# Attention stack as one pipeline over tiles and layers, rotation from PSUM, norms by logarithm

## The chip, the core and the metric

One core of one Trainium2 chip runs the whole program. Five engines work beside each other: PE (TensorE, matrix products and transposes), DVE (VectorE), ACT (ScalarE), POOL (GpSimd) and SP (SyncE, which issues the DMAs here). Each runs its own list of instructions in order and waits on semaphores that others raise. The metric is the time of one execution in microseconds (us); lower is better.

## The reference

The input is 4 batches of 512 tokens with 128 channels, in float32. The model is `x = x + mamba(norm(x))`, then `x = x + stack(norm(x))`, then `x = x + topk_attention(norm(x))`, then `x = x + stack(norm(x))` again with the same weights. Only `stack` concerns the change:

```python
for i in range(6):
    x = attn_layer(shift_tokens(x), Wqkv[i], q_scale[i], k_scale[i], Wo[i]) + x
    x = ffn_layer(shift_tokens(x), ln_g[i], ln_b[i], W1[i], b1[i], W2[i], b2[i]) + x
# attn_layer, 16 heads of 64, windows of 32 tokens; a window sees itself and the one before
q, k = l2norm(q) * qs, l2norm(k) * ksc
q = q * cos * scale + rotate_half(q) * sin * scale      # k the same, with 1 / scale
out = local_attention(q, k, v)                          # softmax over at most 64 keys
# ffn_layer: a norm over the channels, 128 -> 2 x 341, a * gelu(gate), 341 -> 128
```

`shift_tokens` takes the second half of the channels from the token before. `l2norm` divides the 64 numbers of a head by the root of the sum of their squares.

## The kernel before, in words

`ffn_stack` (line 334) is called twice, as f0 and f1, with all activations resident in SBUF (channels on the partitions: `XA` holds a layer's input, `XB` its value after attention). A layer has 16 tiles of 128 tokens, 4 in each batch. In every engine's program `steps` (line 380) runs through the tiles: 4 steps written out, a hardware loop of three rounds of 4 steps, and 3 steps at the end. In the step `kk` four tiles are in work at four stages: projection, rotation and norm of tile `kk`; turning (transposing) of Q and K and the scores of tile `kk-1`; softmax, product with V and division of tile `kk-2`; output projection and residual of tile `kk-3`.

In one step:

- PE projects Q, K and V in six units of 512 columns through PSUM banks 0 and 1 in turn (line 454 for Q and K, 460 for V), multiplies with Wo (line 492), turns prob (465) and Q and K (473), forms PV (line 527) into banks 6 and 7 and the scores (536, 541) into banks 4 and 5, and turns the attention output (551). All turns go through banks 2 and 3.
- ACT copies each unit and each turned bank to SBUF (line 600, `raw`, `v_tok`, `probT`, `qT`, `kT`, `oT`), squares Q and K (619), makes the exponential (645) and the shifted input of the next tile (704, 705).
- DVE rotates from the copies: cos times `raw` (line 771) and sin times `raw` with its halves exchanged (775, two instructions of 512); it sums the squares (797), finds the inverse root by a shifted integer guess and three Newton rounds on 128x32 (754 to 764), sums the softmax (783), divides (808), finds the row maximum (816) and subtracts it (819).
- POOL adds the two halves of the rotation (879), multiplies by the inverse root (882) and adds the residual (874).
- SP issues 20 small DMAs per tile that spread V over the windows, and four weight loads per layer.

When all 16 tiles of a layer are through, the feed-forward part of the layer runs by itself: DVE makes `xn`, the norm's mean, variance and inverse root pass through PE, ACT (Square and Sqrt) and DVE, then for each batch three pairs of products (line 579), Gelu on ACT (726), a product on DVE (854), the output products (565), and DVE adds bias and `XB` into `XA` (844). ACT changes its function table at each of Sqrt, Gelu and Exp (line 719 and its neighbours). The next layer starts when this is over.

Of the kernel before, what the change touches and what calls it, by code (L numbers as in the profile page):

```python
# [333 lines left out]
def ffn_stack(k, a, phase):
    nc = k.nc
    with ExitStack() as ctx:
        s = names(ctx, phase, nc, *LN_SEMS, "wqkv_in", "wo_in", "w12_in", "tabled", "zeroed", "xs_ready", "proj_full", "proj_evac", "v_in_even", "v_in_odd",
                  "sq_done", "ss_done", "newton", "rn_ready", "rope_added", "rot_done", "add_done", "t_full",
                  "t_evac", "scores", "top", "sub_done", "exp_done", "summed", "rden_done", "pv_done", "on_done",
                  "wo_done", "res_done", "shifted", "gate_full", "gate_evac", "val_full", "val_evac", "out_full", "out_evac", "scrap")  # L340
# [29 lines left out]
        warm = sb("warm", [P, 1])  # L370

        xn = raw[:, :, :, :].rearrange("p a h e -> p (a h e)").rearrange("p (b n) -> p b n", b=B)
        k.ln_sq = sq[:, 0, :, :].rearrange("p h e -> p (h e)").rearrange("p (i n) -> p i n", i=2)
        k.ln_std = sq[:, 1, 0:4, :].rearrange("p h e -> p (h e)").rearrange("p (i n) -> p i n", i=2)
        gate = t2[:, 0, :, :].rearrange("p h e -> p (h e)").rearrange("p (i n) -> p i n", i=2)
        hid = rope[:, :, :, :, :].rearrange("p a c h e -> p (a c h e)").rearrange("p (i c n) -> p i c n", i=2, c=4)
# [3 lines left out]
        def steps(eng, fn, L):  # L380

            for j in range(4):
                fn(L, 0, j, j)
            with eng.Fori(1, B) as b:
                for j in range(4):
                    fn(L, b, j, 4 * b + j)
            for j in range(3):
                fn(L, B, j, LT + j)

        def tile(x, r0, r1, b, t0, n=P):  # L390
            if isinstance(b, int):
                return x[r0:r1, b, t0:t0 + n]
# [1236 lines left out]
```

## Time and profile before

| | us |
|---|---|
| median of 3 runs | 7111.84 (7104.78 to 7119.3) |
| profiled execution | 7122.96, of which the span is 7121.2 |
| PE busy | 5984.3 (84%) |
| DVE busy | 5970.1 (84%) |
| ACT busy | 3439.2 (48%) |
| POOL busy | 2652.3 (37%) |
| mean granted clock of TensorE | 0.931 of full |

Busy time is that of one engine, so the columns overlap; the span is the time from the first instruction to the last. The two stacks take most of the span, and in each of them six layers with the same two stages (attention steps, then the feed-forward part) alternate. PEclk is the clock that TensorE was granted: 1.00 is 2.4 GHz, 0.50 is 1.2 GHz. An idle time in brackets names the instruction whose end released the waiting one.

### The profile page before, as it was taken

The page shows a single profiled execution, that of the slowest core. Times are in us where ns is not written, and L with a number is a line of the kernel's source. Part 1 is how long each engine was busy: PE and PEld are TensorE (multiplying, and loading weights), DVE is VectorE, ACT ScalarE, POOL GpSimd, SP SyncE. Part 2 cuts the span into 40 slices and gives each one's busy share as a digit, 9 for nine tenths or more (in the row PEclk, how much of TensorE's full clock was granted, in tenths as well). Part 3 has the DMA queues.
Part 4 walks back from the last instruction along what each step waited for, and adds up shares of the span by engine and source line. Part 5 has one row for each costly group of instructions (what it writes and reads, how often), then busy time and mean ns, then how long its engine had stood idle before and what let it go on. Part 6 is the DMA issues. An engine that isn't in the chain of part 4 may idle for free. (4 is left out here: it accounts for less than half of the span.)

```text
span 7121.2 us, 150074 instructions
## 1 busy us (share of the span) xinstructions
PE 5984.3 (84%) x47596; PEld 3842.3 (54%) x47596; DVE 5970.1 (84%) x12264; ACT 3439.2 (48%) x6820; POOL 2652.3 (37%) x1391
## 2 busy tenths in 40 slices
PE   5777888888888887988988988986888888888888
PEld 1224555555555554565565566565555555555555
DVE  5988888888888885998998998996979797979796
ACT  3335666666666662222222222222657575656565
POOL 1444444444444441122122122221535353535353
PEclk7998999999999998998998998988999999999999
DMA  0002222222222210000000000000212121212121
GB/s 14 0 0 63 59 52 59 52 59 52 59 52 59 53 46 13 1 1 1 1 1 1 1 1 1 1 0 16 60 50 61 51 60 51 63 49 62 50 63 37
DMA packets 159623, 244.44 MB, mean 34 GB/s; under 512 B 36596, under 2 KB 57008, under 8 KB 157494
## 3 DMA queue, kind: packets, MB, share of 16 engines
q1 hardware_dynamic: 159158, 238.71, 13.3%
q8 instruction: 235, 3.85, 0.2%
q14 instruction: 230, 1.88, 0.1%
HBM read 36.20 MB, written 1.05 MB: 5 GB/s over the span
## 5 line engine op out<-in xcount | busy, mean ns | idle before, releaser
L879 POOL TENSOR_TENSOR f_rope<-f_rope,f_t 128x1024 f32<-128x1024 f32 x384 | 918.5, 2392 | 1247.7 <-DVE f_t L775 1247.7
L1315 PE MATMUL psum<-tk_kT,tk_qs 128*128 128x512 f32 (+3 forms) x4128 | 1263.7, 467 | 9.1 <-POOL tk_qs L1548 9.1
L882 POOL TENSOR_TENSOR f_rope<-f_rope,f_rn 128x1024 f32<-128x1024 f32 x384 | 903.7, 2353 | 778.3 <-DVE f_rn L762 763.3
L1548 POOL TENSOR_TENSOR tk_qs<-tk_qT,tk_mix 128x1024 f32<-128x1024 f32 x258 | 499.2, 1938 | 1587.5 <-PE psum L1316 1423.2
L1315 PEld LDWEIGHTS psum<-tk_kT,tk_qs 128*128 128x128 f32 x4128 | 757.3, 208 | 440.5 <-issue 298.4
L775 DVE TENSOR_TENSOR f_t<-f_raw,f_rot 128x512 f32<-128x512 f32 x768 | 903.0, 1214 | 0.0
L454 PE MATMUL psum<-f_wqkv,f_xs 128*128 128x512 f32 x1536 | 785.0, 619 | 104.2 <-DMA f_wqkv<-in_Wqkv 56.1
L1505 DVE MAX8 tk_m<-tk_work 128x8 f32<-128x528 f32 (+3 forms) x1792 | 818.4, 497 | 2.0 <-DVE tk_work L1511 1.5
L1511 DVE MATCH_REPLACE8 tk_work<-tk_m,tk_work 128x400 f32<-128x400 f32 (+3 forms) x1536 | 745.3, 492 | 1.3 <-issue 1.0
L771 DVE TENSOR_TENSOR f_rope<-f_raw,f_rot 128x1024 f32<-128x1024 f32 x384 | 582.9, 1518 | 20.7 <-ACT f_raw L600 19.6
L600 ACT ACTIVATE f_raw<-psum 128x512 f32<-128x512 f32 x768 | 454.6, 595 | 249.2 <-PE psum L454 209.4
L473 PEld LDWEIGHTS psum<-ident,f_rope 128*128 128x128 f32 x3072 | 352.5, 144 | 351.5 <-ACT f_qT L600 218.1
L797 DVE TENSOR_REDUCE f_ss<-f_sq 128x16 f32<-128x1024 f32 x384 | 464.2, 1212 | 75.6 <-ACT f_sq L619 75.6
L1432 ACT ACTIVATE tk_o_tok<-psum,tk_rden 128x64 f32<-128x64 f32 (+1 forms) x256 | 80.3, 314 | 868.7 <-DVE tk_rden L1489 868.7
L473 PE MATMUL psum<-ident,f_rope 128*128 128x128 f32 x3072 | 433.1, 285 | 76.8 <-ACT f_qT L600 65.3
L600 ACT ACTIVATE f_kT<-psum 64x512 f32<-64x512 f32 (+1 forms) x960 | 485.4, 526 | 20.3 <-PE psum L473 10.7
L600 ACT ACTIVATE f_oT<-psum 128x512 f32<-128x512 f32 x384 | 208.4, 594 | 529.1 <-PE psum L551 529.1
L460 PE MATMUL psum<-f_wqkv,f_xs 128*128 128x512 f32 x768 | 409.5, 618 | 43.8 <-ACT f_raw L600 43.0
L492 PEld LDWEIGHTS psum<-f_oT,f_wo 128*128 128x128 f32 x3072 | 384.6, 198 | 109.7 <-issue 74.6
L465 PE MATMUL psum<-ident,f_prob 128*128 128x128 f32 x1536 | 249.4, 290 | 211.6 <-ACT f_wo_sb L600 132.4
L465 PEld LDWEIGHTS psum<-ident,f_prob 128*128 128x128 f32 x1536 | 184.1, 146 | 448.2 <-ACT f_wo_sb L600 250.9
L492 PE MATMUL psum<-f_oT,f_wo 128*128 128x128 f32 x3072 | 393.0, 283 | 26.6 <-ACT f_oT L600 26.6
(234 smaller groups left out, 10764.0 us busy)
## 6 DMA issues: line engine op xcount, KB each, us to landing
f_v<-f_v_tok SPq DMA_DIRECT2D x1152, 128.0 KB, 2.4
f_v<-f_v_tok SPq DMA_DIRECT2D x768, 64.0 KB, 2.0
f_wqkv<-in_Wqkv SPq DMA_DIRECT2D x12, 1536.0 KB, 6.7
f_wo<-in_Wo SPq DMA_DIRECT2D x12, 512.0 KB, 4.1
f_w<-in_W SPq DMA_DIRECT2D x12, 341.0 KB
f_w<-in_W SPq DMA_DIRECT2D x24, 64.0 KB
tk_wkv<-in_Wkv SPq DMA_DIRECT2D x1, 1024.0 KB, 6.0
out<-y_tok SPq DMA_DIRECT2D x4, 256.0 KB, 2.5
```

The lines of the kernel that those rows point to most:

```text
L454: unit(L, kk, n, lambda bank: pe.matmul(bank, xs[:, p, :], wqkv[:, 512 * n:512 * (n + 1)], start=True, stop=True))
L473: last = pe.transpose(psum[:, bank, c * P:(c + 1) * P], rope[:, (j - 1) % 2, n // 2, h:h + 2, :].rearrange("p h e -> p (h e)"), k.ident[:, :])
L492: last = pe.matmul(psum[:, bank, 0:P], wo[:, c, :], oT[:, c, :], start=(c == 0), stop=(c == PAIRS - 1))
L600: return act.activation(out, psum[:, bank, :] if source is None else source, ACT.Copy)
L771: dve.tensor_tensor(rope[:, j % 2, half, :, :], raw[:, half, :, :], cos, ALU.mult)
L775: last = dve.tensor_tensor(t2[:, half, :, hd * q:hd * (q + 1)], raw[:, half, :, hd * (1 - q):hd * (2 - q)], sin, ALU.mult)
L879: pool.tensor_tensor(part, part, t2[:, half, :, :], ALU.add).then_inc(s["rope_added"], 1)
L882: pool.tensor_tensor(part, part, rn[:, H * half:H * (half + 1)].unsqueeze(2).to_broadcast([P, H, DH]), ALU.mult).then_inc(s["add_done"], 1)
L1315: pe.matmul(psum[:, j, 0:n], qs[:, j, c, :], kT[:, c, 0:n], start=(c == 0), stop=False, skip_group_check=True)
L1505: dve.max(m8[:, j, 8 * r:8 * r + 8], src(j)).then_inc(s["m8"], 1)
L1511: dve.match_replace(work[:, j, 0:n], m8[:, j, 8 * r:8 * r + 8], src(j), REMOVED).then_inc(s["removed"], 1)
L1548: pool.tensor_tensor(qs[:, j, :, :], qT[:, :, P * t:P * (t + 1)], mix[:, :, heads(p, j)].to_broadcast([P, PAIRS, P]), ALU.mult).then_inc(s ...
```

## The change

Six layers of 16 tiles become one run of 96 tiles. `groups` takes the place of `steps`: a group is the four steps of one batch; layer 0 is written out, a hardware loop runs the other five layers with 16 steps in each round, and two groups follow at the end. The attention tiles of the next layer enter the pipeline while those of this layer are still in it. The feed-forward of a batch is cut into four pieces, one for each step of the group that comes two groups after the batch's attention group. Step j=0 has the shifted copy, the mean, centring, square and variance; j=1 has the inverse root, its spreading over the partitions, scale and gain; j=2 has the three pairs of products with Gelu; j=3 has the output product and the sum into `XA`.

The copies `raw` go: the K projection fills banks 0 and 1 as a pair, ACT squares it and DVE rotates it straight from PSUM, one instruction for cos and one for sin; then the Q projection uses the same banks. V, Wo and the feed-forward share banks 6 and 7, and PV shares banks 4 and 5 with the scores. The integer guess and the Newton rounds on DVE go. POOL makes the maximum with 1e-24, ACT makes Ln and Exp with the factor -0.5, and POOL polishes with one Newton round in four instructions. The norm of the feed-forward is made in the same way on 128x128. ACT has Square, Copy, Ln and Exp in one table and loads another for Gelu once in a group. Wqkv comes in three DMAs of 512 KB.

```diff
+        def groups(eng, group):
+
+            for b in range(B):
+                group(0, b, 4 * b, (0, b - 2) if b >= 2 else None)
+            with eng.Fori(1, LAYERS) as L:
+                for b in range(B):
+                    group(L, b, LT * L + 4 * b, (L, b - 2) if b >= 2 else (L - 1, b + 2))
+            for b in range(2):
+                group(LAYERS, b, STACK + 4 * b, (LAYERS - 1, b + 2))
...
+                    def project(which, sem):
+                        for n in range(2):
+                            last = pe.matmul(psum[:, n, :], xs[:, j % 2, :], wqkv[:, INNER * which + 512 * n:INNER * which + 512 * (n + 1)], start=True, stop=True)
...
+                    def gated(c):
+                        h0, m = HCH[c]
+                        n = 3 * f + c
...
+                        wait(pe, "gate_evac", n)
+                        pe.matmul(psum[0:m, F0, :], w1[:, HID + h0:HID + h0 + m], xn[:, :], start=True, stop=True).then_inc(s["gate_full"], 1)
...
+                    if on(g, 0):
+                        if first:
+                            pe.wait_ge(s["wk_in"], 1 + 16 * (L + 1))
+                        wait(pe, "q_rot", through(g, 1))
+                        pe.wait_ge(s["xs_ready"], 1 + g + 1)
+                        project(1, "k_full")
...
+                    if on(g, 1):
+                        wait(pe, "k_normed", through(g, 1))
...
+                    if on(g, 0):
+                        if first:
+                            pe.wait_ge(s["wq_in"], 1 + 16 * (L + 1))
+                        pe.wait_ge(s["k_rot"], 1 + g + 1)
+                        project(0, "q_full")
...
+                        gated(2)
+
...
+                    def output():
+                        if on(g, 3):
...
+                    if j != 2:
+                        output()
...
+                    if j == 2:
+                        output()
...
-                    def copy_qk(n):
-                        if on(kk, 0):
-                            act.wait_ge(s["proj_full"], 1 + QKV_UNITS * g0 + n + 1)
-                            if n % 2 == 0:
-                                act.wait_ge(s["rot_done"], 1 + 2 * g0 + n // 2 + 1)
-                            evac(raw[:, n // 2, 8 * (n % 2):8 * (n % 2) + 8, :].rearrange("p h e -> p (h e)"), n % 2).then_inc(s["proj_evac"], 1)
...
+                    if f is not None and j == 2:
+                        gelu(1)
+                    if on(g, 0):
+                        wait(act, "q_ss", through(g, 1))
+                        wait(act, "q_full", g + 1)
+                        act.activation(sq[:, 0, :, :], qk_bank, ACT.Square).then_inc(s["q_sq"], 1)
...
+                    if f is not None and j == 2:
+                        gelu(2)
+                        act.preload_act_table_set(EXP_LN)
...
+                        wait(act, "res_done", through(g, 4))
+                        wait(act, "wo_full", through(g, 3))
+                        copy(wo_sb[:, :], psum[:, F0, 0:P]).then_inc(s["wo_evac"], 1)
+                    if on(g, 0):
+                        wait(act, "x_ready", g + 1)
+                        act.activation(nt[:, 1, :], nt[:, 0, :], ACT.Ln).then_inc(s["logged"], 1)
+                        wait(act, "logged", g + 1)
+                        act.activation(nt[:, 2, :], nt[:, 1, :], ACT.Exp, scale=-0.5).then_inc(s["y_ready"], 1)
+                    if on(g, 2):
+                        wait(act, "wo_full", through(g, 3))
+                        for n in range(2):
+                            wait(act, f"ot{n}_full", through(g, 2))
+                            copy(flat4(oT, n), psum[:, T0 + n, :]).then_inc(s[f"ot{n}_evac"], 1)
...
-                        wait_alone(dve, s["newton"], NEWTON * g + at[0], s["scrap"]) if at[0] == 2 else dve.wait_ge(s["newton"], 1 + NEWTON * g + at[0])
-
-                    x, h, y, z = (nt[:, n, :] for n in range(4))
...
-                    for n in range(3):
-                        link(dve.scalar_tensor_tensor(z, y, -0.5, y, ALU.mult, ALU.mult))
-                        link(dve.tensor_tensor(h, z, x, ALU.mult))
...
+                def rotate(g, j, half, name):
+
+                    dve.wait_ge(s[f"{name}_sq"], 1 + g + 1)
+                    for n in range(2):
+                        wait(dve, f"{name}t{n}_full", through(g, 2))
+                    cos = rot[:, half, j, :].unsqueeze(1).to_broadcast([P, H, DH])
+                    dve.tensor_tensor(rope[:, j % 2, half, :, :], qk_bank, cos, ALU.mult)
+                    wait(dve, f"{name}_added", through(g, 1))
+                    sin = rot[:, 2 + half, j, :].rearrange("p (q e) -> p q e", q=2).unsqueeze(1).to_broadcast([P, H, 2, hd])
+                    swapped = qk_bank.rearrange("p h (q e) -> p h q e", q=2)[:, :, ::-1, :]
+                    dve.tensor_tensor(t2[:, half, :, :].rearrange("p h (q e) -> p h q e", q=2), swapped, sin, ALU.mult).then_inc(s[f"{name}_rot"], 1)
+                    wait(dve, "x_ready", through(g, 1))
+                    dve.tensor_reduce(ss[:, H * half:H * (half + 1)], sq[:, half, :, :], AX_X, ALU.add).then_inc(s[f"{name}_ss"], 1)
...
+                def polished(dst, x, y, z, h, sem, base, done):
+
+                    pool.tensor_tensor(z, y, y, ALU.mult).then_inc(s[sem], 1)
+                    wait(pool, sem, base + 1)
+                    pool.tensor_tensor(h, z, x, ALU.mult).then_inc(s[sem], 1)
+                    wait_apart(pool, sem, base + 2)
+                    pool.tensor_scalar(z, h, -0.5, 1.5, ALU.mult, ALU.add).then_inc(s[sem], 1)
+                    wait(pool, sem, base + 3)
+                    pool.tensor_tensor(dst, y, z, ALU.mult).then_inc(s[done], 1)
...
+                    def norm(half, name):
+                        part = rope[:, j % 2, half, :, :]
+                        pool.wait_ge(s[f"{name}_added"], 1 + g + 1)
+                        pool.tensor_tensor(part, part, rn[:, H * half:H * (half + 1)].unsqueeze(2).to_broadcast([P, H, DH]),
+                                           ALU.mult).then_inc(s[f"{name}_normed"], 1)
...
+                    if on(g, 0):
+                        add(1, "k")
+                    if on(g, 3):
...
+                        wait(pool, "wo_evac", through(g, 3))
+                        pool.tensor_tensor(k.XB[:, bb, t0:t0 + P], wo_sb[:, :], k.XA[:, bb, t0:t0 + P], ALU.add).then_inc(s["res_done"], 1)
+                    if on(g, 0):
+                        add(0, "q")
+                        pool.wait_ge(s["k_ss"], 1 + g + 1)
+                        wait_apart(pool, "q_ss", g + 1)
+                        pool.tensor_scalar(nt[:, 0, :], ss[:, :], 1e-24, None, ALU.max).then_inc(s["x_ready"], 1)
+                        pool.wait_ge(s["y_ready"], 1 + g + 1)
+                        polished(rn[:, :], nt[:, 0, :], nt[:, 2, :], nt[:, 3, :], nt[:, 4, :], "polish", 3 * g, "rn_ready")
+                        pool.wait_ge(s["rn_ready"], 1 + g + 1)
+                        norm(1, "k")
+                        norm(0, "q")
```

PE, the end of a step and the start of the next in the kernel before (`ISA` and `REGISTER_ALU` hold waits and addresses):

```order
L527 MATMUL psum<-f_v,f_probT 32x128 x32
L533 REGISTER_ALU
L534 REGISTER_ALU
L536 MATMUL psum<-band,ident_bf 128x512 x2
L541 MATMUL psum<-f_kT,f_qT 32x128 x32
L440 ISA
L551 MATMUL psum<-ident,f_o_tok 128x128 x4
L440 ISA
L551 MATMUL psum<-ident,f_o_tok 128x128 x4
L480 ISA
L445 ISA
L454 MATMUL psum<-f_wqkv,f_xs 128x512
```

The same engine in the third step of a group in the changed kernel (`f_xn`, `f_w` are the feed-forward's input and first weight):

```order
L491 MATMUL psum<-f_xn,f_w 128x512
L496 MATMUL psum<-f_xn,f_w 128x512
L473 MATMUL psum<-f_wqkv,f_xs 128x512 x2
L464 MATMUL psum<-ident,f_rope 128x128 x8
L394 REGISTER_ALU
L491 MATMUL psum<-f_xn,f_w 85x512
L496 MATMUL psum<-f_xn,f_w 85x512
L600 MATMUL psum<-band,ident_bf 128x512 x2
L605 MATMUL psum<-f_kT,f_qT 32x128 x32
L394 REGISTER_ALU
L587 MATMUL psum<-f_oT,f_wo 128x128 x8
L464 MATMUL psum<-ident,f_o_tok 128x128 x8
```

The Q projection now stands between the second and the third pair of feed-forward products, and the scores stand ahead of the product with Wo; in the other three steps Wo comes first.

POOL, one step of the kernel before, with its waits:

```order
L879 TENSOR_TENSOR f_rope<-f_rope,f_t 128x1024 [waits f0_rot_done]
L880 REGISTER_ALU
L881 REGISTER_ALU [waits f0_rope_added]
L882 TENSOR_TENSOR f_rope<-f_rope,f_rn 128x1024 [waits f0_rn_ready]
L877 REGISTER_ALU
L879 TENSOR_TENSOR f_rope<-f_rope,f_t 128x1024 [waits f0_rot_done]
L880 REGISTER_ALU
L882 TENSOR_TENSOR f_rope<-f_rope,f_rn 128x1024 [waits f0_rn_ready,f0_rope_added]
```

And one step of the changed kernel (`f_nt` holds the argument and the steps of the inverse root, `f_rn` its result):

```order
L862 TENSOR_TENSOR f_rope<-f_rope,f_t 128x1024 [waits f0_k_rot]
L880 TENSOR_TENSOR XB<-f_wo_sb,XA 128x128 [waits f0_wo_evac]
L862 TENSOR_TENSOR f_rope<-f_rope,f_t 128x1024 [waits f0_q_rot]
L885 TENSOR_SCALAR f_nt<-f_ss 128x32 [waits f0_k_ss,f0_q_ss]
L848 TENSOR_TENSOR f_nt<-f_nt 128x32 [waits f0_y_ready]
L850 TENSOR_TENSOR f_nt<-f_nt 128x32 [waits f0_polish]
L852 TENSOR_SCALAR f_nt<-f_nt 128x32 [waits f0_polish]
L854 TENSOR_TENSOR f_rn<-f_nt 128x32 [waits f0_polish]
L867 TENSOR_TENSOR f_rope<-f_rope,f_rn 128x1024 [waits f0_k_added,f0_rn_ready]
L867 TENSOR_TENSOR f_rope<-f_rope,f_rn 128x1024 [waits f0_q_added]
```

Both additions, the residual and the small instructions now stand ahead of the first multiplication by the inverse root.

## Rows read from the trace of the kernel before

**Rows 1.** Windows: start and end; length; busy of PE, PEld, DVE, ACT, POOL; PEclk.
```profile
1010.00:1148.00 138.00, 123.69 (x1519) 84.99 (x1519) 132.36 (x201) 101.65 (x184) 81.52 (x41) 1.00 0.25 61
...
1198.00:1278.00 80.00, 65.45 (x436) 37.85 (x437) 37.07 (x52) 27.64 (x48) 5.57 (x5) 0.94 0.12 37
```
**Rows 2.** Timeline: start, length; first projection, last output of both stacks.
```profile
567.80 3.78 PE L454 MATMUL psum<-f_wqkv,f_xs 128*128 128x512 f32 x4 [28.22 <-DMA f_wqkv<-in_Wqkv]
...
2692.37 0.75 DVE L844 SCALAR_TENSOR_TENSOR XA<-psum,b,XB 128x512 f32<-128x512 f32 x1 [2.94 <-PE psum L565]
...
4982.85 2.07 PE L454 MATMUL psum<-f_wqkv,f_xs 128*128 128x512 f32 x2 [27.92 <-DMA f_wqkv<-in_Wqkv]
...
7105.61 0.75 DVE L844 SCALAR_TENSOR_TENSOR XA<-psum,b,XB 128x512 f32<-128x512 f32 x1 [2.94 <-PE psum L565]
```
**Rows 3.** Groups of instructions, 1010 to 1150 us, DVE and POOL: busy, mean ns, idle.
```profile
L775 DVE TENSOR_TENSOR f_t<-f_raw,f_rot 128x512 f32<-128x512 f32 x32 | 36.0, 1163 | 0.0
...
L771 DVE TENSOR_TENSOR f_rope<-f_raw,f_rot 128x1024 f32<-128x1024 f32 x17 | 26.3, 1547 | 0.0
...
L797 DVE TENSOR_REDUCE f_ss<-f_sq 128x16 f32<-128x1024 f32 x16 | 19.4, 1213 | 2.4 <-ACT f_sq L619 2.4
...
L819 DVE TENSOR_TENSOR f_prob<-psum,f_top 128x1024 f32<-128x1024 f32 x9 | 11.0, 1225 | 0.3
...
L758 DVE SCALAR_TENSOR_TENSOR f_nt<-f_nt 128x32 f32<-128x32 f32 x24 | 4.6, 192 | 1.0 <-DVE f_nt L764 0.3
...
L879 POOL TENSOR_TENSOR f_rope<-f_rope,f_t 128x1024 f32<-128x1024 f32 x17 | 40.2, 2366 | 26.3 <-DVE f_t L775 26.3
```
**Rows 4.** Groups, same stretch, ACT.
```profile
L619 ACT ACTIVATE f_sq<-f_raw 128x1024 f32<-128x1024 f32 x17 | 17.9, 1053 | 0.3
...
L600 ACT ACTIVATE f_kT<-psum 64x512 f32<-64x512 f32 x32 | 18.8, 589 | 0.3
```
**Rows 5.** Timeline of one steady step, PE, with the hand-offs.
```profile
1105.27 1.96 PE L527 MATMUL psum<-f_v,f_probT 128*32 128x128 f32 x64
...
1108.68 1.90 POOL L882 TENSOR_TENSOR f_rope<-f_rope,f_rn 128x1024 f32<-128x1024 f32 x1 [3.97 <-DVE f_rn L762]
...
1108.18 0.60 PE L536 MATMUL psum<-band,ident_bf 128*128 128x512 bf16 x2 [0.95 <-ACT f_kT L600]
...
1108.71 1.96 PE L541 MATMUL psum<-f_kT,f_qT 128*32 128x128 f32 x64
...
1110.60 1.09 PE L551 MATMUL psum<-ident,f_o_tok 128*128 128x128 f32 x8
...
1111.52 1.88 PE L454 MATMUL psum<-f_wqkv,f_xs 128*128 128x512 f32 x4
...
1113.24 1.95 PE L492 MATMUL psum<-f_oT,f_wo 128*128 128x128 f32 x16
...
1116.53 0.65 PE L465 MATMUL psum<-ident,f_prob 128*128 128x128 f32 x4 [0.48 <-ACT f_wo_sb L600]
...
1117.02 1.02 PE L454 MATMUL psum<-f_wqkv,f_xs 128*128 128x512 f32 x2
```
**Rows 6.** Groups, whole run: nearest rows for what the change adds.
```profile
L1555 POOL TENSOR_TENSOR X<-tk_y,X 128x128 f32 x16 | 7.0, 435 | 199.0 <-ACT tk_y L1442 199.0
...
L237 POOL TENSOR_SCALAR_AFFINE_SELECT mask_f<-mask_f 32x64 f32<-32x64 f32 x4 | 0.9, 233 | 0.6
...
L719 ACT ACT_TABLE_LOAD x12 | 15.4, 1283 | 0.2
...
L156 DVE TENSOR_TENSOR f_raw<-f_raw,psum 128x512 f32<-128x512 f32 x48 | 30.9, 644 | 8.9 <-PE psum L123 8.8
```
**Rows 7.** Timeline: TensorE after an idle stretch of 4.60 us.
```profile
1666.29 1.11 PE L465 MATMUL psum<-ident,f_prob 128*128 128x128 f32 x4 [4.60 <-ACT f_prob L645]
...
1667.19 1.91 PE L454 MATMUL psum<-f_wqkv,f_xs 128*128 128x512 f32 x2
```
**Rows 8.** Windows in the top-k stage, columns as in Rows 1.
```profile
3052.00:3056.00 4.00, 4.00 (x12) 2.97 (x13) 4.00 (x13) 0.00 (x0) 0.00 (x0) 0.50 0.00 0
```

More of the change, by code:

```diff
@@ L369, in ffn_stack @@
         wo_sb = sb("wo_sb", [P, P])
[L370 to L376, printed above, removed]
@@ L378, in ffn_stack @@
-        psum = k.psum
[L380 to L392, printed above, removed]
-            return x[r0:r1, ds(b, 1), t0:t0 + n].rearrange("p o n -> p (o n)")
+        xn = sb("xn", [P, N])
@@ new lines, in step @@
+                    if f is not None and j == 2:
+                        gated(1)
+                    if f is not None and j == 3:
+                        pe.wait_ge(s["w2_in"], 1 + 16 * 3 * (ff[0] + 1))
+                        wait(pe, "v1_evac", through(g, 0))
+                        wait(pe, "val_evac", 3 * f + 3)
+                        for c, (h0, m) in enumerate(HCH):
+                            last = pe.matmul(psum[:, F1, :], w2[0:m, c, :], hid[0:m, c, :], start=(c == 0), stop=(c == 2))
+                        last.then_inc(s["out_full"], 1)
@@ new lines, in step @@
+                    if on(g, 0):
+                        if first:
+                            pe.wait_ge(s["wq_in"], 1 + 16 * (L + 1))
+                        pe.wait_ge(s["k_rot"], 1 + g + 1)
+                        project(0, "q_full")
+                    if on(g, 1):
+                        wait(pe, "q_normed", through(g, 1))
+                        for n in range(2):
+                            wait(pe, f"kt{n}_evac", through(g, 1))
+                            turn(T0 + n, rope[:, (j - 1) % 2, 0, :, :], 8 * n, f"qt{n}_full")
@@ L585, in _ @@
-                with pe.Fori(0, LAYERS) as L:
-                    steps(pe, step, L)
-                    feed_forward(L)
+                            if on(g, 1):
+                                wait(pe, f"qt{n}_evac", through(g, 1))
+                            else:
+                                wait(pe, f"pt{n}_evac", through(g, 2))
+                            turn(T0 + n, o_tok, 8 * n, f"ot{n}_full")
+                    if f is not None and j == 0:
+                        wait(pe, "ff_squared", f + 1)
+                        for n in range(TILES):
+                            last = pe.matmul(psum[WIN * n:WIN * (n + 1), F1, 0:P], k.mean_w[:, 0:WIN], ffsq[:, P * n:P * (n + 1)], start=True, stop=True)
+                        last.then_inc(s["ff_var"], 1)
@@ L714, in _ @@
[L714 to L729 removed]
+                                    copy(kT[rows, 4 * n:4 * n + 4, par, 0:WIN], turned[rows, :, P - WIN:P])
@@ new lines, in step @@
+                    if f is not None and j == 0:
+                        wait(act, "ff_var", f)
+                        wait(act, "ff_centred", f + 1)
+                        act.activation(ffsq[:, :], xn[:, :], ACT.Square).then_inc(s["ff_squared"], 1)
+                    if on(g, 1):
+                        for n in range(2):
+                            wait(act, f"qt{n}_full", through(g, 1))
+                            copy(flat4(qT, n), psum[:, T0 + n, :]).then_inc(s[f"qt{n}_evac"], 1)
@@ L732, in _ @@
+                groups(act, group)
             @block.vector
@@ new lines, in group, with layer_vec, layer_col, layer_row @@
+                def group(L, b, g, ff):
+                    for j in range(4):
+                        step(L, b, j, g + j, ff)
+                groups(pool, group)
+def layer_vec(x, L):
+    return x[:, L:L + 1] if isinstance(L, int) else x[:, ds(L, 1)]
+def layer_col(x, L, m, which, c):
+    return x[0:m, L, which, c:c + 1] if isinstance(L, int) else x[0:m, ds(L, 1), which, c]
+def layer_row(x, half, L, e0, e1):
+    return x[:, half, L:L + 1, e0:e1] if isinstance(L, int) else x[:, half, ds(L, 1), e0:e1]
```

665 lines of the change are left out of this document (294 added, 371 removed).

## The prediction

> **What bounds the kernel now.** I read the page's busy shares first, then the windows, the groups of a steady stretch, and last one step of it in the timeline. The page gives PE and DVE 84% each, which says nothing of a stage. The windows do [rows 1]: 1010 to 1148 us holds eight attention steps, with DVE busy 132.36 of 138 us (96%), PE 123.69 (90%) and the clock at 1.00. A step takes 17.3 us and DVE sets it. From 1198 to 1278 us stands the feed-forward part: PE 65.45 of 80, DVE 37.07, ACT 27.64, POOL 5.57, so nobody is full and attention waits. A stack lasts from the first projection to the last sum, 567.80 to 2693.12, and 4982.85 to 7106.36 [rows 2]: 2125.3 and 2123.5 us, or 354.2 per layer. 16 x 17.3 = 277 of it is steps, so fill, drain and feed-forward take 77. The sum is made for one stack of 2124.4 and counted twice, against the profiled 7122.96 (span 7121.2, which is 11 above the median of 7111.84; I subtract from 7113 to forecast the median).
>
> **DVE is relieved.** Now a step spends 16.5 us of DVE (132.36 / 8). The sin product from SBUF costs 1.163 per 512 and the cos product 1.547 per 1024 [rows 3]; in the step shown the neighbours cost far less from PSUM: the subtraction with a PSUM source is 1.225 per 1024, and stays so. The change makes four products of 1024 from PSUM: 4 x 1.22 = 4.9, for 2 x 1.547 + 4 x 1.163 = 7.7. A sin product with exchanged halves from PSUM is not in the trace. Bounds: 1.22 (PSUM source, 1024) and 2.33 (the two of 512 now); below 1.22 nothing of 1024 elements lies. I take 1.22, the row with the same source and size. Eleven small Newton operations (0.192 each with gaps, 2.6 us [rows 3]) go. There remain 4.9, two sums of squares 2 x 1.21, softmax sum, division, maximum and subtraction, 4 x 1.22, and the reciprocal 0.24: 12.4. The feed-forward adds per batch two products of 512 from PSUM at 0.644 [rows 6], three with the shape and source of a 0.75 row, and the last sum of 0.75 [rows 2]: 4.3, over four steps 1.1. DVE has 13.5 of work in a step, and is no longer the bound.
>
> **What bounds it then: a chain over four engines.** Q cannot be projected before DVE has read K out of banks 0 and 1, and the next Exp cannot start before the norm's Ln and Exp, which stand ahead of it in ACT's list. I follow the chain from the end of one softmax Exp to the end of the next. PE: turn prob, project V, turn K, PV, project Q. From starts in the timeline [rows 5] a turn of eight is 1111.52 - 1110.60 = 0.9, two projections 1113.24 - 1111.52 = 1.7, and 64 window products 1110.60 - 1108.71 = 1.9: 0.9 + 1.7 + 0.9 + 1.9 + 1.7 = 7.1, and a hand-off of 0.25, an estimate within the 0.48 that PE stood after ACT's copy at 1116.53. ACT squares Q: 1.05 [rows 4]. DVE makes cos and sin: 2.44. POOL adds: 2.36 [rows 3], and takes the maximum. ACT makes Ln and Exp on 128x32, copies two banks of oT (2 x 0.55), and makes Exp, 1.05 like Square. Small operations on POOL are not in the trace at this shape: 0.233 for 32x64 and 0.435 for 128x128 bound them [rows 6]; I take 0.25, since 32 columns stand nearer the first. A small one on DVE is 0.192, and ACT's are taken like it, so Ln and Exp are 0.5 with hand-offs, and further hand-offs 0.5. Sum: 7.1 + 0.25 + 1.05 + 2.44 + 2.61 + 0.5 + 1.1 + 1.05 + 0.5 = 16.6 us. PE works beside DVE and POOL in turn Q, Wo, scores and turn o (0.9 + 1.75 + 2.4 + 0.9 = 6.0, with 0.5 for the band [rows 5]) and ends 0.5 to 1 before the norm. It then waits for Exp 1.3 to 1.6 us. The POOL polish (4 x 0.25) and two multiplications (the second at 1.90 [rows 5]) end before the K turn in the next step, which they have 5 us to reach, so they cost nothing.
>
> **Feed-forward inside.** In j=0 the mean product adds 0.85 on PE's part of the chain and a square on ACT 0.7: 18.1. In j=1 the spreading adds 0.9 and the gain 0.65: 18.1. In j=2 two pairs of products (2 x 1.7) come before the Q projection, with a wait of 1.25 in which DVE divides (1.22) and makes the hidden product; then turn Q 0.9, the third pair 1.7, scores 2.4, and only then Wo 1.75. ACT's Exp for the norm waits for the Wo copy (0.25 + 0.26), and POOL's maximum waits behind the residual (0.45) and the addition of Q (2.36), which stands behind that residual: 7.1 + 3.4 + 1.25 + 0.9 + 1.7 + 2.4 + 1.75 + 0.25 + 0.26 + 0.45 + 2.61 + 0.5 + 1.1 + 1.05 + 0.5 = 25.2. Two table loads of 1.283 [rows 6] lie on ACT while PE and POOL work; without that cover they would cost 2.6 a group. In j=3 the output product adds 3 x 0.85: 19.1. A group takes 18.1 + 18.1 + 25.2 + 19.1 = 80.5, say 81 us, or 324 a layer against 354.2. PE waits for Exp 1.3, 1.6, 2.3 and 3.9 us in the steps, longest in j=3, because after j=2 its list is done while POOL and ACT still have the residual, addition, norm and Exp before them.
>
> **The stack.** Of the 24 batches 22 groups carry feed-forward: 22 x 81 = 1782. Two groups of plain steps at the start: 8 x 16.6 = 133. At the end the last batches stand alone: some 35 for the last attention steps and 22 for a lone chain of norm, Gelu and output, 57. Weight waits and the loop's edge at each layer: 5 x 2 = 10. Together 1982, so 142 less per stack, 284 for two. The first K projection waits for 512 KB of weights and not for 1536 KB, behind which it stands idle now [rows 2]; I take 2.5 us off each stack, an estimate between nothing and a tenth of the 28 us of that wait. At full clock this gives 7113 - 289 = 6824.
>
> **TensorE's clock.** After an idle stretch of 4.60 us a turn of four takes 1.11 and two 512-column records 1.91 [rows 7], where the same take 0.65 and 1.02 in the steady step [rows 5]: at half clock for about 3 us, which costs 1.5. In the top-k stage stretches at 0.50 stand without any idle time of PE around them [rows 8], 9.6 us in a row, and there the cost would be 4.8. The 3.9 us wait in j=3 is between the 1.3 of today and 4.60. I take 2 us for each group, near the row with an idle stretch ahead: 2 x 22 x 2 = 88. Range: 0 to 4.8, or 0 to 211. Forecast: 6824 + 88 = 6912, say 6915.
>
> The Trainium skill, "TensorE: Matmul & The Clock Gate", section "HAM oscillation — how this bites in real kernels", says that idle gaps between bursts of matmuls put the clock back to half, each time anew, although the work is unchanged. That speaks against this change, which turns a full DVE queue into gaps on PE; by it the waits of each j=3 step would be followed by slow work, and the result of that is rival D. The trace agrees for one gap of 4.60 us and is silent on gaps from 1.6 to 3.9.
>
> **Rivals.**
> - B: the clock stays at 1.00 through gaps of 3.9: 6824. For it: 1.3 and 1.6 us gaps are there now at 1.00. Against: 4.60 drops it.
> - C: TensorE becomes the bound, the waits are covered. Work of PE is 15.5 in a step [rows 1] less overlap, 15.1 by the starts, plus 9.6 a batch over four steps (2.4): 96 x 17.5 = 1680, with 40 of drain 1720: 7113 - 808 = 6305. Against: the orders of ACT and POOL tie Exp to the norm.
> - D, slower: half clock after each gap that lasts on through PE's part of the chain. PE has some 38 us on the chain in a group, and half of it at half clock costs 19: 22 x 19 x 2 = 836, 7660. It decides from 142 / 22 = 6.5 us lost in a group.
> - E: unseen prices go the bad way. The sin product takes 2.33 from PSUM; of the two only part lies on the chain, about 2.1 a group with its effect on K, 46 a stack. Small POOL operations at 0.6 add 1.9 a group, 42 a stack. One or both: 7005 to 7090.
> - F: the chain in j=2 and at layer edges is longer by 6 us a group than I find, and the time stays within 0.2%.
>
> **Numbers.** Forecast 0.45, B 0.20, E 0.15, D 0.13, C 0.04, F 0.03. Faster than 0.2% (14 us, what a measurement of this kernel can tell): 0.45 + 0.20 + 0.15 + 0.04 = 0.84; same 0.03; slower 0.13. The range goes from 6760 (below B by 60, for gaps that cost nothing and a shorter j=2) to 7120 (E with both prices); it leaves out D and C, 0.17.
>
> **What would show it.** Right: step pitches near 18, 18, 25 and 19 us; DVE busy 13.5 a step; cos and sin at 1.22; ACT waiting some 3 us a step on POOL's maximum ahead of Ln; PE waiting up to 3.9 us for Exp in j=3; clock 0.95 or more in the stacks. Wrong: sin at 2.3, POOL's small ones above 0.5, a clock near 0.75 (D), equal pitches near 17.5 with PE full (C), or a group above 87 us, at which nothing is gained.

## The result and the profile after

The changed kernel takes 6860.74 us (median of 4 runs, 6845.46 to 6865.6) against 7112.7: ratio 0.9642, 95% interval 0.9628 to 0.9656, so 252 us or 3.6% less. The forecast was 6915 in a range of 6760 to 7120, and faster with a chance of 0.84. The profiled execution has a span of 6856.4 us. DVE is busy 4954.1 us (72%, before 84%), PE 86%, ACT 47%, POOL 39%; the mean granted clock is 0.934, before 0.931.

Windows of the changed kernel, columns as in [rows 1] (the third number from the end is the clock): one group of four steps from the end of a softmax Exp to the same place one group on, and the whole first stack.

```profile
1557.97:1637.45 79.48, 71.47 (x796) 47.99 (x796) 52.24 (x50) 50.20 (x97) 42.08 (x45) 1.00 0.23 61
...
563.87:2563.48 1999.61, 1766.77 (x19104) 1177.01 (x19104) 1262.20 (x1230) 1210.89 (x2304) 1011.47 (x1056) 0.97 0.23 59
```

Below, the pitch of a step is the time from the softmax Exp that opens it to the one that opens the next. A group of four steps takes 79.48 us. DVE has 52.24 of work in it, 13.1 a step where it had 16.5. PE has 71.47 (90%). The first stack takes 1999.6 us where it took 2125.3 [rows 2]. Its ends and two marks in it, in the timeline (start, length; Exp at 697.30 and 2501.45): the first projection, the softmax Exp that opens the first step with feed-forward work, the one that closes the last such group, and the last sum.

```profile
563.87 3.78 PE L473 MATMUL psum<-f_wqkv,f_xs 128*128 128x512 f32 x4 [26.55 <-DMA f_wqkv<-in_Wqkv]
...
697.30 1.06 ACT L656 ACTIVATE f_prob<-f_prob 128x1024 f32<-128x1024 f32 x1
...
2501.45 1.06 ACT L656 ACTIVATE f_prob<-f_prob 128x1024 f32<-128x1024 f32 x1
...
2562.73 0.75 DVE L824 SCALAR_TENSOR_TENSOR XA<-psum,b,XB 128x512 f32<-128x512 f32 x1 [3.00 <-PE psum L561]
```

So 133.4 us go to the first eight steps, 1804.2 to the 22 groups, and 62.0 to the end. The second stack, from 4848.66 to 6840.54, takes 1991.9. The groups of instructions from 1010 to 1150 us, the stretch of [rows 3]:

```profile
L777 DVE TENSOR_TENSOR f_rope<-psum,f_rot 128x1024 f32<-128x1024 f32 x14 | 17.1, 1225 | 15.9 <-ACT f_sq L707 13.8 <-ACT f_sq L674 2.1
...
L781 DVE TENSOR_TENSOR f_t<-psum,f_rot 128x1024 f32<-128x1024 f32 x14 | 17.0, 1215 | 0.0
...
L862 POOL TENSOR_TENSOR f_rope<-f_rope,f_t 128x1024 f32<-128x1024 f32 x14 | 33.1, 2362 | 4.5 <-DVE f_t L781 4.4
...
L867 POOL TENSOR_TENSOR f_rope<-f_rope,f_rn 128x1024 f32<-128x1024 f32 x14 | 26.4, 1905 | 0.6
...
L885 POOL TENSOR_SCALAR f_nt<-f_ss 128x32 f32<-128x32 f32 x7 | 2.0, 285 | 0.6
...
L854 POOL TENSOR_TENSOR f_rn<-f_nt 128x32 f32<-128x32 f32 x7 | 1.8, 253 | 0.6
```

The cos product is 1.225 per 1024 where it was 1.547, and the sin product 1.215 for 1024 where it was 1.163 for 512. POOL's addition costs what it did (2.362), its multiplication 1.905, and the small instructions 0.285 and 0.253.

The chain of the step with j=2, in the timeline of all engines:

```profile
1576.69 1.23 DVE L836 TENSOR_TENSOR f_prob<-psum,f_top 128x1024 f32<-128x1024 f32 x1
...
1577.22 0.28 ACT L634 ACTIVATE f_wo_sb<-psum 128x128 f32<-128x128 f32 x1 [2.38 <-PE psum L587]
...
1577.58 0.46 POOL L880 TENSOR_TENSOR XB<-f_wo_sb,XA 128x128 f32<-128x128 f32 x1 [13.35 <-ACT f_wo_sb L634]
...
1577.99 2.34 POOL L862 TENSOR_TENSOR f_rope<-f_rope,f_t 128x1024 f32<-128x1024 f32 x1
...
1580.41 0.28 POOL L885 TENSOR_SCALAR f_nt<-f_ss 128x32 f32<-128x32 f32 x1
...
1580.73 0.23 ACT L735 ACTIVATE f_nt<-f_nt 128x32 f32<-128x32 f32 x1 [3.23 <-POOL f_nt L885]
...
1582.08 1.06 ACT L656 ACTIVATE f_prob<-f_prob 128x1024 f32<-128x1024 f32 x1
...
1583.19 1.09 PE L464 MATMUL psum<-ident,f_prob 128*128 128x128 f32 x8 [3.48 <-ACT f_prob L656]
```

DVE is done with the subtraction at 1577.92, and Exp (ACT L656) starts only at 1582.08. Between stand ACT's copy of Wo's result, POOL's residual (L880) and addition of Q (L862), the maximum (L885), ACT's Ln and small Exp, and two oT copies. PE then stands idle for 3.48 us.

### The profile page after: what moved, and what is told of

It reads as the page before. It is cut to its first block and busy times, and to the rows that moved or that the text cites. A ratio compares the mean times of both kernels' runs of the same rounds, so it can differ in the third digit from the quotient of the medians.

```text
span 6856.4 us, 139904 instructions
## 1 busy us (share of the span) xinstructions
PE 5881.8 (86%) x47596; PEld 3844.7 (56%) x47596; DVE 4954.1 (72%) x9384; ACT 3189.4 (47%) x6666; POOL 2706.0 (39%) x2543
## 3 DMA queue, kind: packets, MB, share of 16 engines
HBM read 36.20 MB, written 1.05 MB: 5 GB/s over the span
## 5 line engine op out<-in xcount | busy, mean ns | idle before, releaser
L862 POOL TENSOR_TENSOR f_rope<-f_rope,f_t 128x1024 f32<-128x1024 f32 x384 | 907.4, 2363 | 296.2 <-DVE f_t L781 293.8
L473 PE MATMUL psum<-f_wqkv,f_xs 128*128 128x512 f32 x1536 | 750.3, 612 | 104.3 <-DMA f_wqkv<-in_Wqkv 55.3
L777 DVE TENSOR_TENSOR f_rope<-psum,f_rot 128x1024 f32<-128x1024 f32 x384 | 469.1, 1222 | 448.7 <-ACT f_sq L707 376.0
L867 POOL TENSOR_TENSOR f_rope<-f_rope,f_rn 128x1024 f32<-128x1024 f32 x384 | 723.6, 1905 | 15.1
L880 POOL TENSOR_TENSOR XB<-f_wo_sb,XA 128x128 f32<-128x128 f32 x192 | 83.9, 437 | 1478.8 <-ACT f_wo_sb L634 1478.8
L800 DVE TENSOR_REDUCE f_den<-f_prob 128x16 f32<-128x1024 f32 x192 | 234.3, 1220 | 464.5 <-ACT f_prob L656 464.5
L473 PEld LDWEIGHTS psum<-f_wqkv,f_xs 128*128 128x128 f32 x1536 | 276.8, 194 | 376.0 <-issue 313.8
L781 DVE TENSOR_TENSOR f_t<-psum,f_rot 128x1024 f32<-128x1024 f32 x384 | 466.6, 1215 | 0.0
L707 ACT ACTIVATE f_sq<-psum 128x1024 f32<-128x1024 f32 x192 | 196.8, 1025 | 517.5 <-PE psum L473 517.5
L812 DVE TENSOR_TENSOR f_o_tok<-psum,f_rden 128x1024 f32<-128x1024 f32 x192 | 235.1, 1225 | 271.4 <-PE psum L539 271.4
L464 PE MATMUL psum<-ident,f_rope 128*128 128x128 f32 x3072 | 403.6, 275 | 3.2 <-POOL f_rope L867 2.6
```

Source lines behind the costliest of these rows:

```text
L464: last = pe.transpose(psum[:, bank, c * P:(c + 1) * P], src[:, h:h + 2, :].rearrange("p h e -> p (h e)"), k.ident[:, :])
L473: last = pe.matmul(psum[:, n, :], xs[:, j % 2, :], wqkv[:, INNER * which + 512 * n:INNER * which + 512 * (n + 1)], start=True, stop=True)
L777: dve.tensor_tensor(rope[:, j % 2, half, :, :], qk_bank, cos, ALU.mult)
L781: dve.tensor_tensor(t2[:, half, :, :].rearrange("p h (q e) -> p h q e", q=2), swapped, sin, ALU.mult).then_inc(s[f"{name}_rot"], 1)
L862: pool.tensor_tensor(part, part, t2[:, half, :, :], ALU.add).then_inc(s[f"{name}_added"], 1)
L867: pool.tensor_tensor(part, part, rn[:, H * half:H * (half + 1)].unsqueeze(2).to_broadcast([P, H, DH]), ALU.mult).then_inc(s[f"{name}_norme ...
```

## The experiments

All edits are to the changed kernel. Ratios are to the kernel before, of runs on the same chip as each; the changed kernel's own is 0.9642. Differences in us are between medians taken on different chips, on which the kernel before took 7103.5 to 7112.7, so each can be off by up to 20 us; where it matters, the difference by the ratios stands beside.

**Rotation from SBUF again (a_undo_rot).**

```diff
+ act.activation(raw[:, :, :], qk_bank, ACT.Copy).then_inc(s["k_raw"], 1)   # the same for Q
- dve.tensor_tensor(rope[:, j % 2, half, :, :], qk_bank, cos, ALU.mult)
+ dve.tensor_tensor(rope[:, j % 2, half, :, :], raw[:, :, :], cos, ALU.mult)
# sin: two instructions of 512 that read raw
```

> ACT copies each projection (K, then Q) to SBUF, and DVE rotates from the copy, as before the change (cos 1024, sin 2 x 512); the rest is as changed. Theory (rotation from PSUM shortens the chain over PE, ACT, DVE and POOL, since two-input SBUF operations are slow beside POOL): cos and sin of Q together 3.5 to 5 us and not 2.44, so 1.1 to 2.6 a step in 192 steps, 7080 to 7360 us, likeliest 7220. Rival (DVE has slack, and reading PSUM gains nothing): 6860 to 6890.

Measured: 7133.63 us, ratio 1.0042 (1.0029 to 1.0055). Groups of its trace, 1010 to 1150 us:

```profile
L780 DVE TENSOR_TENSOR f_rope<-f_raw,f_rot 128x1024 f32<-128x1024 f32 x13 | 25.9, 1994 | 13.7 <-ACT f_raw L709 11.9 <-ACT f_raw L675 1.7
...
L786 DVE TENSOR_TENSOR f_t<-f_raw,f_rot 128x512 f32<-128x512 f32 x26 | 17.1, 699 | 0.0
```

Cos takes 1.994 and the two halves of sin 1.4, together 3.4 where PSUM gave 2.44. The four pitches go from 17.7, 17.7, 25.2 and 18.9 to 19.6, 19.9, 26.0 and 19.5 to 22.5. One part of the change thus carries 273 us (284 by the ratios), more than the whole gain. The rival falls. What it is made of is shown only in part: Q's rotation lies on the chain, and a rotation grew by 0.95 on average, while the pitches with j=0 and j=1 grew by 1.8 and 2.2. K's rotation is longer too, and ACT has two more copies of 1.02 in each step; the edit does not separate these.

**Newton rounds back on DVE (b_newton).**

```diff
+ newton(g)     # DVE, behind the subtraction; the 11 instructions of before
- act.activation(nt[:, 1, :], nt[:, 0, :], ACT.Ln) ... ACT.Exp, scale=-0.5
- pool.tensor_scalar(nt[:, 0, :], ss[:, :], 1e-24, None, ALU.max) ... polished(rn, ...)
```

> The inverse root of Q and K goes back to DVE (shifted guess, three Newton rounds, 11 small instructions), behind the subtraction of the row maximum; ACT makes no Ln and Exp for it and POOL no maximum and polish. Theory (the softmax Exp stands behind the norm's Ln and Exp in ACT's list, and this sets the step with j=2): that step goes from 25.2 to about 22, the wait of 3.5 us on PE after it shrinks and with it the clock loss of 1.7, while in the other steps the turn of K waits up to 0.9 longer for its norm: 6750 us, between 6700 and 6900. Rival (the logarithm pays because it takes work from DVE): 2.6 a step more, 192 x 2.6 = 500, 7360 us.

Measured: 6929.13 us, ratio 0.9751 (0.9734 to 0.9767), 68 slower than the changed kernel (78 by the ratios), and outside the 6700 to 6900 expected. Half the theory stands: j=2 fell from 25.2 to 22.9 us. But the other steps rose to 18.5, 19.0 and 21 or more, above what I gave them. PE's timeline shows the reason: the turn of K now waits for its norm on POOL, 0.80 us in most steps, and 2.1 to 2.4 in those with j=3.

```profile
1393.41 1.09 PE L464 MATMUL psum<-ident,f_rope 128*128 128x128 f32 x8 [0.80 <-POOL f_rope L888]
...
1429.78 2.35 POOL L883 TENSOR_TENSOR f_rope<-f_rope,f_t 128x1024 f32<-128x1024 f32 x1
1429.89 2.28 DVE L848 TENSOR_SCALAR f_nt<-f_nt 128x32 uint32<-128x32 uint32 x1
...
1436.73 1.09 PE L464 MATMUL psum<-ident,f_rope 128*128 128x128 f32 x8 [2.22 <-POOL f_rope L888]
```

At the end of j=2 DVE's shift for the guess (L848) starts 0.11 us behind POOL's addition of Q and ends with it: 2.28 us, where it takes 0.18 in the other steps. So the norm comes late and the turn of K in j=3 waits for it. In 15 of the 34 steps with j=3 away from an edge the pitch is 22.6 to 23.0 and not 21.1, at a clock of 0.92 to 0.93 where the others have 1.00.

**More DVE work beside the chain (c_off_chain), and on it (d_on_chain).**

```diff
+ dve.tensor_copy(spare[:, :, :], sq[:, 1, :, :])                 # c: behind the sum of K's squares
+ if half == 0: dve.tensor_tensor(spare[:, :, :], qk_bank, cos, ALU.mult)   # d: ahead of Q's cos product
```

> One extra copy of 128x1024 from SBUF to SBUF on DVE in each step, behind the sum of K's squares, where DVE then idles. Theory (DVE is not the bound): 6861 to 6885 us. Rival (DVE's work sets the step): 192 times the length of the copy, 0.6 to 1.1, so 6975 to 7070.

> The cos product of Q is made twice on DVE (the first result goes to a spare buffer): 1.14 us more between Q's square and POOL's addition. Theory (that place lies on the chain that sets the step): 192 x 1.14 = 219 more, 7080 us, at least 7030. Rival (the chain is another, such as PE's own list): under 50 more, 6910.

Measured: c 6864.86 us, ratio 0.9653 (0.9636 to 0.967); d 7033.23 us, ratio 0.9898 (0.9875 to 0.9922). The copy of c was longer than I thought:

```profile
L808 DVE COPY f_spare<-f_sq 128x1024 f32<-128x1024 f32 x5 | 10.6, 2127 | 0.0
```

192 x 2.127 = 408 us of time added to DVE moved the time by 4 (8 by the ratios, the intervals overlap). In d 192 x 1.14 = 219 us added moved it by 172. DVE's amount of work does not bound the kernel, the place in the chain does. The pitches of d say where that place is on the chain: at full clock they are 18.45, 18.3, 25.15 and 20.0, so 0.7, 0.65, nothing and 1.1 more. In j=2 nothing comes of it, since there POOL's addition of Q waits for the residual. That is 2.45 a group, 108 us in 44 groups. Most of the rest of the 172 is slow work of PE, whose gaps are longer too: of the 44 steps with j=2, which a gap of 2.22 now opens, 25 took 26.7 to 27.1, at a clock of 0.94.

**Residual behind the maximum (h2_late_res), and Wo ahead of the scores in j=2 (j_wo_first).**

```diff
# h, POOL
  add(1, "k")
- residual
  add(0, "q")
  pool.tensor_scalar(nt[:, 0, :], ss[:, :], 1e-24, None, ALU.max)
+ residual
# j, PE: output() always stands ahead of the scores
```

> POOL adds the residual behind the addition of Q and the maximum, and not ahead of them. Theory (in j=2 Exp comes 4.1 us after the subtraction because the late product with Wo holds the residual, and that holds Q's addition and the maximum): Exp 3.1 us earlier in j=2, PE's gap under 1 us and so no clock loss in j=3, (3.1 + 1.2) x 44 = 189 less, 6670 us, between 6640 and 6760. Rival (PE's order holds the step): 6850 to 6861.

> In the step with j=2 the product with Wo comes before the scores, as in the other steps; POOL's order is as changed. Theory (the late Wo holds the residual, Q's addition, the norm and Exp): Exp 2.3 us earlier in j=2, as then the scores are 1.75 later, and no clock loss of about 1.1 a group: 3.4 x 44 = 150 less, 6711 us, between 6690 and 6780. Rival (the place of Wo does not matter, only POOL's): 6850 or more.

Measured: h 6638.29 us, ratio 0.9339 (0.9323 to 0.9355); j 6702.02 us, ratio 0.9447 (0.9426 to 0.9467). The timeline of h at the place shown above for the changed kernel:

```profile
1594.38 0.28 POOL L880 TENSOR_SCALAR f_nt<-f_ss 128x32 f32<-128x32 f32 x1
...
1594.79 1.23 DVE L836 TENSOR_TENSOR f_prob<-psum,f_top 128x1024 f32<-128x1024 f32 x1
...
1595.32 0.28 ACT L634 ACTIVATE f_wo_sb<-psum 128x128 f32<-128x128 f32 x1 [2.39 <-PE psum L587]
...
1595.62 0.23 ACT L735 ACTIVATE f_nt<-f_nt 128x32 f32<-128x32 f32 x1
...
1595.68 0.41 POOL L885 TENSOR_TENSOR XB<-f_wo_sb,XA 128x128 f32<-128x128 f32 x1 [1.02 <-ACT f_wo_sb L634]
...
1596.97 1.06 ACT L656 ACTIVATE f_prob<-f_prob 128x1024 f32<-128x1024 f32 x1
...
1598.08 1.09 PE L464 MATMUL psum<-ident,f_prob 128*128 128x128 f32 x8 [0.27 <-ACT f_prob L656]
```

The maximum (L880 here) is done at 1594.66, before the subtraction begins. Exp now waits for the Wo copy and oT, 0.95 us behind the subtraction and not 4.1, and PE's gap is 0.27. Its j=2 pitch is 21.98 and not 25.15. In j it is 23.1. Both edits cut the same chain from two sides, and both came within 32 us of the number worked out; h came out 2 us below its range, in part since the pitch with j=1 also fell, from 17.65 to 17.2. The two edits together were not tried.

**Filling PE's gap (e2_clock_fill).** The extra products are not used.

```diff
+ if j == 3 and f is not None:
+     wait(pe, "val_evac", 3 * f + 3)
+     for n in range(2): pe.matmul(psum[:, F1, :], xs[...], wqkv[...], start=True, stop=True)
```

> In each step with j=3 two extra projections (1.71 us, result unused) on PE ahead of its wait for Exp, which was 3.48 us. Theory (that idle time costs the clock, about 1.7 us of slow work behind it in two groups of three): the gap is 1.8, the pitch is 18.9 in all groups, about 28 x 1.7 = 48 less, 6815 us. Rival (the clock falls for another reason): 6861, or 6935 if the extra products delay the chain.

Measured: 6813.86 us, ratio 0.9581 (0.9565 to 0.9597). In the changed kernel the gap of 3.48 us is followed by slow work in some groups (four records of the V projection, 3.54 us) and not in others (1.88):

```profile
1495.28 1.18 PE L464 MATMUL psum<-ident,f_prob 128*128 128x128 f32 x8 [3.48 <-ACT f_prob L656]
...
1496.25 3.54 PE L523 MATMUL psum<-f_wqkv,f_xs 128*128 128x512 f32 x4
```

```profile
1584.12 1.88 PE L523 MATMUL psum<-f_wqkv,f_xs 128*128 128x512 f32 x4
```

The granted clock of the two places (third number from the end):

```profile
1497.00:1499.00 2.00, 2.00 (x4) 0.85 (x3) 2.00 (x3) 0.72 (x2) 1.55 (x1) 0.50 0.00 0
1584.00:1586.00 2.00, 2.00 (x9) 0.99 (x8) 1.97 (x4) 1.62 (x4) 2.00 (x2) 1.00 0.00 0
```

With the gap filled to 1.77 us (L507 is the extra work) it is always 1.88, and away from the layer edges all 34 pitches of j=3 lie between 18.87 and 18.90:

```profile
1564.01 1.88 PE L507 MATMUL psum<-f_wqkv,f_xs 128*128 128x512 f32 x4
...
1567.66 1.09 PE L464 MATMUL psum<-ident,f_prob 128*128 128x128 f32 x8 [1.77 <-ACT f_prob L660]
...
1568.59 1.88 PE L527 MATMUL psum<-f_wqkv,f_xs 128*128 128x512 f32 x4
```

More work on PE made the kernel 47 us faster (43 by the ratios). By the Trainium skill, "TensorE: Matmul & The Clock Gate", section "HAM oscillation — how this bites in real kernels", idle gaps between bursts bring half clock; the trace agrees for 3.48 us, but in only 11 of the 17 gaps of the first stack that lie away from an edge, and in 9 of 17 in the second.

**The layer edge (f2_early_w, g2_unrolled).** The pitches at the four edges of the first stack that hold a jump of the loop sum to 42.8 to 46.0 us for two steps, against 36.6 elsewhere; in the second stack it is 42.2 to 44.4. All engines of the changed kernel show it:

```profile
1509.71 0.36 SPq L430 DMA_DIRECT2D f_wqkv<-in_Wqkv  x1
...
1511.95 1.09 PE L464 MATMUL psum<-ident,f_o_tok 128*128 128x128 f32 x8
...
1513.80 1.07 ACT L634 ACTIVATE f_oT<-psum 128x512 f32<-128x512 f32 x2
...
1517.06 1.06 ACT L656 ACTIVATE f_prob<-f_prob 128x1024 f32<-128x1024 f32 x1 [2.19 <-issue]
...
1518.43 3.77 PE L473 MATMUL psum<-f_wqkv,f_xs 128*128 128x512 f32 x4 [5.39 <-issue]
```

SP issues the weights (L430) at 1509.71, ACT resumes at 1517.06 "from issue", that is with nothing seen that held it, and PE at 1518.43. The clock is at half by then:

```profile
1518.00:1520.00 2.00, 1.57 (x2) 0.83 (x3) 1.81 (x4) 1.26 (x3) 1.14 (x1) 0.50 0.05 12
```

```diff
# f, SP: the next layer's K and V weights are issued ahead of spread_v of tile 15, those of Q behind it
# g, PE, ACT, DVE, POOL
- with eng.Fori(1, LAYERS) as L:
+ for L in range(1, LAYERS):
```

> The three parts of the next layer's Wqkv are issued around the spreading of V of the layer's last tile, not behind it and the loop's edge. A layer edge costs 8.4 us over two ordinary steps, ten times. Theory (the engines wait there for their own instructions behind the loop's jump, not for weights): 6850 to 6861 us. Rival (late weights): 84 less, 6777.

> The layer loop is written out on PE, ACT, DVE and POOL; SP keeps its loop. Theory (the jump and the loading of code cost the 8.4 us at each edge): up to 84 less, 6777 to 6800 us. Rival (late weights): 6861, since these come as before.

Measured: f 6844.42 us, ratio 0.9627 (0.9611 to 0.9643); g 6819.2 us, ratio 0.9593 (0.9577 to 0.9609). The jump carries most of it: without it the gain is 42 us (35 by the ratios), against 16 for the weights, whose interval overlaps the changed kernel's. The traces agree: over 36.6 each, the eight edges with a jump cost 61 us in the changed kernel, 40 in f and 14 in g. So both edits did something and neither did what was expected: f lies 6 us below its theory and far from its rival, g 19 above its range. I had counted ten edges of 8.4; eight hold a jump, at 7.6, and g keeps 1.7 of clock loss at five of them, so 84 was too much. Whether the jump itself costs this or the fetching of the code behind it, g does not separate. In g, with the jump gone, the weights are what PE waits for next, 0.64 us:

```profile
1501.31 1.09 PE L464 MATMUL psum<-ident,f_o_tok 128*128 128x128 f32 x8
...
1503.05 1.98 PE L473 MATMUL psum<-f_wqkv,f_xs 128*128 128x512 f32 x4 [0.64 <-DMA f_wqkv<-in_Wqkv]
```

**Both arithmetic parts undone (p_pipeline_only).** The edits of a and b together.

> Both arithmetic parts are undone together: DVE rotates from SBUF copies and makes the Newton rounds (behind the subtraction); what is left of the change is the pipeline over tiles and layers with the feed-forward in the steps, in its order of work. Theory (the pipeline moves feed-forward work into a step that DVE already fills, so it gives nothing without the relief): 7130 to 7350 us, likeliest 7200. Rival (the pipeline by itself gives back the 77 us of each layer's end): under 7000 us.

Measured: 7253.15 us, ratio 1.0207 (1.019 to 1.0224). Its windows, 1350 to 1450 us, and two waits of PE, in j=3 and in j=1:

```profile
1350.00:1450.00 100.00, 84.44 (x939) 55.37 (x932) 81.20 (x116) 62.45 (x108) 47.41 (x28) 0.98 0.23 59
```

```profile
1416.33 1.09 PE L465 MATMUL psum<-ident,f_rope 128*128 128x128 f32 x8 [2.10 <-POOL f_rope L894]
...
1462.19 1.13 PE L553 MATMUL psum<-f_std,row_w 128*128 128x128 f32 x8 [2.66 <-POOL f_std L881]
```

The pipeline alone makes the kernel 2.1% slower. The number came out, the reason I gave did not: DVE is at 81%, not full. A group takes 88.6 us (19.7, 23.2, 23.8 and 21.9 for j=0 to 3), PE waits 2.10 for the norm of K in j=3 and 2.66 for the norm of the feed-forward in j=1, and no engine is full: by that the chain has grown longer, which I did not test further.

**A faster version (m_combined).** h, f and g together.

> Three edits together: residual behind the maximum on POOL, next layer's Wqkv issued early, and the layer loop written out on PE, ACT, DVE and POOL. Theory (an edge waits for the jump and for the weights, and either alone hides the other's share): 6638 less 42, 16 and what is left of the 8.4 us at ten edges, 6565 us, between 6550 and 6590. Rival (the shares only add): 6580 or more, and if code loading bites in the longer program, 6638.

Measured: 6606.87 us (6585.55 to 6622.59), ratio 0.931 (0.9287 to 0.9333). Below h by 31, not by the 73 expected, outside the range of 6550 to 6590, and its interval overlaps that of h, so a gain over h is likely but not shown by the times alone. The profiled run, span 6583.7, has almost nothing left at the edges: 18.9 and 18.3 us for the two steps, 0.6 over elsewhere. The eight edges stand 46 us above their ordinary steps in h's trace and 5 in this one, so the edges had 41 to give; the theory that either edit hides the other's share is wrong. The four timed runs spread over 37 us, from 6585.55, the profiled one, to 6622.59, and why stays open. Its first stack, 575 to 2450 us:

```profile
575.00:2450.00 1875.00, 1729.62 (x19158) 1157.80 (x19156) 1268.58 (x1240) 1209.81 (x2302) 1006.65 (x1049) 0.99 0.24 63
```

PE is busy 92% of that stretch, at a clock of 0.99.

## Why the prediction was right

**The bound.** That the amount of DVE's work no longer sets the time, and a chain over four engines does, is shown: 408 us more beside the chain cost 4, 219 on it cost 172 (about 108 of it by the chain, most of the rest by slow work of PE), and taking POOL's residual out of it gave 222 (215 by the ratios). That DVE set the step before rests on its 96% [rows 1] alone.

**The terms, per stack, against the trace.** First eight steps: 133 forecast, 133.4 measured, in part by chance: the plain pitch is 16.3 and not 16.6, the first Exp comes after 30.0 and not two pitches of 16.6, but the last two steps take 20.3 and 17.9. The first of these has j=2, where the late Wo holds the step even without feed-forward work (in run j, with Wo first, it takes 16.3); the prediction gave it the plain pitch. The pitches 18.1, 18.1, 25.2 and 19.1 came out at 17.75, 17.7, 25.2 and 18.9, a group at 79.5 and not 81. That rounding up, from 80.5, and 1.0 us in the terms made 22 x 1.5 = 33 us, the largest error. End: 57 against 62.0. PE waits for the Exp that opens a step 1.1, 0.5, 1.6 and 3.5 us for j=0 to 3; the forecast was 1.3, 1.6, 2.3 and 3.9: the longest is where it was put, and all four are shorter. ACT waits 3.3 us a step for the maximum, as forecast.

**Clock and edges.** Together they were forecast at 44 + 10 = 54 and came to 55, but by chance: the clock cost 20.6 in the first stack away from the edges (11 gaps of 17, nine at 1.7 and two at 2.7), where I took 2 us in each of 22 groups; the edges cost 35, not 10. The step that failed is "Weight waits and the loop's edge at each layer: 5 x 2". It priced the jump at 2 us from no row. That each layer's idle end hid the jump in the kernel before is my reading and was not tested. It is not every jump that costs: in the kernel before the loop inside a layer jumped after every four steps, and the pitches around those jumps are 17.27 like the others (DVE was full there, so a stall of another engine could be hidden).

The upper bound of the clock term rested on a misreading of [rows 8]. The stretch at half clock did have idle time of PE ahead of it, 2.65 us:

```profile
3047.46 0.60 PE L1328 MATMUL psum<-ident,tk_e 128*16 128x128 f32 x4 [2.65 <-DVE tk_e L1516]
```

And the gaps that the steps had at full clock in the kernel before were 0.5 to 1.1 us, not the 1.3 and 1.6 that the prediction names. The gap's length alone does not settle the matter either: of the gaps of 2.22 in d, 25 of the 44 ahead of j=2 were followed by slow work and 2 of those ahead of j=0.

**The unseen prices.** Sin from PSUM with exchanged halves: 1.215, forecast 1.22, so rival E's 2.33 is out. DVE's work in a step: 13.1, forecast 13.5. POOL's small instructions: 0.22 to 0.29, forecast 0.25. The gap in j=3: 3.48, forecast 3.9.

**The sum.** A stack was forecast at 1982 + 44 = 2026 and took 1999.6. Twice the difference is 53, and 6915 - 6861 = 54, but that the two agree is chance: the second stack took 1991.9, 34 below the forecast, and the profiled run of the kernel before lay 10 us above the 7113 that the sum subtracts from. Rival B (full clock, 6824) is wrong on the clock; with the gap filled, which leaves the clock loss at the edges, the kernel took 6814. Rival D's mechanism exists, at 1.7 us a gap where it needed 6.5 a group to decide. Rival C's bound is not reached: PE still waits in every step.

**What the parts are worth.** The prediction took the three parts as one. Undone one by one they give back 273 (rotation) and 68 (norm); undone together 392. The pipeline alone costs 150 against the kernel before on the same chip, so it pays only with the relief. Pipelining with only one of the two was measured as well: 0.9751 with rotation from PSUM, 1.0042 with the logarithm. The relief without the pipeline was not tried.

## What to carry to other kernels

When an engine that was full is relieved, write down the chain from one iteration's marked instruction to the next over all engines, by their lists in order; here it gave the four pitches to 2.5% or better, where busy shares give nothing. Look in that chain for a small instruction (here a residual of 0.45 us) that stands ahead of a critical one in its engine's list but waits for something late: moving it gained 222 us, nearly as much as the whole change. Look also at the two steps around a loop's jump: here they cost 61 us over both stacks, where the forecast had 20.
